# A gated sum formed in TensorE's accumulator banks: two products with the identity per tile in place of a VectorE sum and one transpose

## What is computed

```python
gate = jax.nn.sigmoid(local @ gl_w + remote_h @ gr_w)
mixed = gate * local + (1.0 - gate) * remote_h
mixed = mixed.transpose(0, 2, 1, 3).reshape(B, S, D)
return mixed @ out_w + out_b
```

## Time and profile before

| | |
|---|---|
| median of 3 runs | 1197.87 us (1192.1 to 1199.39) |
| the profiled execution | 1195.67 us, of which the span of instructions is 1193.9 us |
| PE busy (weight loads apart) | 1035.2 us, 87% of the span |
| DVE busy | 930.8 us, 78% |
| POOL busy | 714.8 us, 60% |
| ACT busy | 681.3 us, 57% |
| granted TensorE clock, mean | 0.965 of full speed |
| the chain that ended last | PE 46%, DVE 34%, ACT 8%, issue 6%, POOL 5% |

### The profile page before, as it was taken

The page is one execution under the profiler, slowest core; times in us unless marked ns, Lnnn a source line. Parts: engine busy times, 40 slices in busy tenths (PEclk is TensorE's granted clock), DMA queues, the critical chain, the costliest instruction groups (busy, mean ns, idle before and its releaser), DMA issues.

```text
span 1193.9 us, 38039 instructions
## 1 busy us (share of the span) xinstructions
PE 1035.2 (87%) x15776; PEld 661.3 (55%) x15776; DVE 930.8 (78%) x2148; ACT 681.3 (57%) x1043; POOL 714.8 (60%) x890
## 2 busy tenths in 40 slices
PE   4767899898999999898999989898999989896855
PEld 2435556565656556565656656565655556563533
DVE  5567888889887878879788878888887887975545
ACT  3414566565656566565656566665646656563733
POOL 5406556675656566675665656675655567564744
PEclk9977999999999999999999999999999999996977
DMA  6640241606133250605233160604225060511000
GB/s 219 177 130 3 79 119 41 176 23 166 50 109 91 74 143 32 185 23 145 54 114 103 49 169 32 178 29 126 74 80 137 32 186 23 150 29 39 2 19 18
DMA packets 51272, 108.19 MB, mean 91 GB/s; under 512 B 8054, under 2 KB 35190, under 8 KB 47990
## 3 DMA queue, kind: packets, MB, share of 16 engines
q1 hardware_dynamic: 50460, 105.75, 31.5%
q10 hardware_dynamic: 640, 0.00, 0.0%
HBM read 71.55 MB, written 34.08 MB: 88 GB/s over the span
## 4 chain that ended last, share of the span: by engine, by line
PE 46%; DVE 34%; ACT 8%; issue 6%; POOL 5%; ACTq 0%; DVEq 0%; POOLq 0%
PE oacc L1508 7%; PE oacc L1489 7%; PE work L1565 6%; PE work L1432 5%; PE scores L1469 4%; ACT Pt L793 4%; DVE Pt L979 3%; PE work L1499 3%; DVE nmax L1059 3%; DVE stats L1146 2%; DVE Pt L1017 2%; DVE x L1122 2%; DVE ytok L1140 2%; PE scores L1411 2%; POOL h_lo L664 2%
## 5 line engine op out<-in xcount | busy, mean ns | idle before, releaser
L793 ACT ACTIVATE Pt<-scores 128x1024 f32<-128x1024 f32 (+1 forms) x256 | 228.7, 915 | 116.3 <-PE oacc L1489 75.2
L1059 DVE TENSOR_REDUCE nmax<-work 128x3 f32<-128x480 f32 x352 | 218.2, 637 | 29.5 <-PE work L1437 24.2
L664 POOL TENSOR_TENSOR h_lo<-hbuf,h_hi 128x512 f16<-128x512 f32 x128 | 149.2, 1170 | 133.8 <-DVE h_hi L1181 133.8
L636 POOL TENSOR_SCALAR_AFFINE_SELECT Pt<-Pt 128x512 f32<-128x512 f32 x256 | 166.1, 649 | 95.0 <-ACT Pt L793 93.8
L628 POOL TENSOR_TENSOR parts<-Pt,parts 128x512 bf16<-128x512 f32 x64 | 72.4, 1159 | 142.7 <-ACT parts L743 133.0
L1432 PE MATMUL work<-Ks,Qs 98*32 98x160 bf16 x4096 | 142.0, 236 | 15.2 <-DVE nmax L1059 11.5
L1489 PE MATMUL oacc<-Pt,Vp 128*32 128x256 f32 (+1 forms) x2048 | 149.2, 358 | 4.0 <-POOL Pt L640 3.6
L1508 PE MATMUL oacc<-wdn_t,h_hi 128*128 128x256 f16 x512 | 118.1, 273 | 17.4 <-POOL h_lo L664 17.4
L1469 PE MATMUL scores<-Qs,Ks 100*32 100x160 bf16 (+4 forms) x4096 | 113.9, 228 | 18.9 <-ACT Pt L793 15.9
L640 POOL TENSOR_SCALAR_AFFINE_SELECT Pt<-Pt 128x512 f32<-128x512 f32 x192 | 126.7, 660 | 0.0
L829 ACT ACTIVATE hbuf<-work 128x512 f32<-128x512 f32 x128 | 76.2, 595 | 76.7 <-PE work L1565 61.4
(11 more groups left out here) (169 smaller groups left out, 2078.1 us busy)
## 6 DMA issues: line engine op xcount, KB each, us to landing
parts_scratch<-parts SPq DMA_DIRECT2D x96, 256.0 KB, 5.6
Qs<-parts_scratch SPq DMA_DIRECT2D x96, 256.0 KB, 5.0
Ks<-parts_scratch SPq DMA_DIRECT2D x96, 256.0 KB, 4.7
xtok<-L_attn_x SPq DMA_DIRECT2D x16, 512.0 KB, 6.8
xres<-L_attn_x SPq DMA_DIRECT2D x16, 512.0 KB, 7.7
y<-ytok SPq DMA_DIRECT2D x16, 512.0 KB, 3.3
nat<-L_ffn_w_up SPq DMA_DIRECT2D x1, 1024.0 KB, 8.3
nat<-L_ffn_w_down SPq DMA_DIRECT2D x1, 1024.0 KB, 10.3
```

The source lines that it names most:

```text
L636: ins = pool.affine_select(out=pt[:, :, 0:P], in_=pt[:, :, 0:P], compare_op=ALU.is_gt, fill=0.0, base=0, pattern=[[0, 4], [1, P]], channel ...
L664: pool.tensor_tensor(h_lo[:, t % NR, :], hbuf[:, t % 2, :], h_hi[:, t % NR, :], ALU.subtract).then_inc(h_lo_ready, 1)
L793: nc.scalar.activation(Pt[:, u % NPT, :, 0:w], scores[:, slot, :, :].rearrange("p k (h q) -> p (k h) q", h=2)[:, :, 0:w], ACT.Exp, scale=S ...
L1059: nc.vector.tensor_reduce(nmax[:, :, :].rearrange("p b h -> p (b h)")[:, first:first + n], work[:, slot, 0:n * BAND].rearrange("p (h c) -> ...
```

## The change

VectorE's four sums per sequence are gone, with their semaphore. TensorE waits for `mix_part` in place of `mixed_ready`. For each tile of 128 by 128 it now does two matmuls with the identity as the moving operand, the first with the local part and the second with the remote part as the stationary one. Both go into the same columns of the accumulator: the first with `start=True`, the second adds to it and stops.

```diff
-                    def add_parts(b):
-
-                        dve.wait_ge(mix_part, count(s, NB, b))
-                        nc.vector.tensor_tensor(mixed[:, b, :], mixed[:, b, :], rem[:, s.par, b, 0:D], ALU.add
-                                                ).then_inc(mixed_ready, 1)
-
                     for b in range(NB):
...
-                        if b > 0:
-                            add_parts(b - 1)
-                    add_parts(NB - 1)
...
                     for b in range(NB):
-                        pe.wait_ge(mixed_ready, count(s, NB, b))
+                        pe.wait_ge(mix_part, count(s, NB, b))
                         for t in range(KT):
-                            mm = nc.tensor.transpose(oacc[:, t, b * P:(b + 1) * P],
-                                                     mixed[:, b, t * P:(t + 1) * P], ident[:, :])
+                            cols = slice(t * P, (t + 1) * P)
+                            nc.tensor.matmul(oacc[:, t, b * P:(b + 1) * P], mixed[:, b, cols], ident[:, :],
+                                             start=True, stop=False, skip_group_check=True)
+                            mm = nc.tensor.matmul(oacc[:, t, b * P:(b + 1) * P], rem[:, s.par, b, cols], ident[:, :],
+                                                  start=False, stop=True, skip_group_check=True)
                             if b == NB - 1:
                                 mm.then_inc(mix_T, 1)
```

More of the change, by code:

```diff
@@ L368, in build @@
         xn_lo = sem("xn_lo")
-        mixed_ready = sem("mixed_ready")
         var_ready = sem("var_ready")
```

## The result

| | before | after |
|---|---|---|
| median | 1196.67 us (1192.1 to 1199.39, 4 runs) | 1225.38 us (1221.62 to 1225.78, 4 runs) |
| profiled execution | 1195.67 us, span 1193.9 | 1221.62 us, span 1219.9 |
| PE busy | 1035.2 us | 1071.4 us |
| DVE busy | 930.8 us | 906.3 us |
| chain that ended last | PE 46%, DVE 34% | PE 60%, DVE 23% |

The changed kernel is slower: ratio 1.024 with a 95% interval of 1.020 to 1.028, some 29 us. The forecast was 1229 us, in a range from 1220 to 1246. VectorE has lost the 25 us of work that the change took from it, and TensorE has 36 us more. The profiled execution of the changed kernel is the fastest of its four, so the two traces lie 26 us apart where the medians lie 28.7 apart.

The account below looks back on a forecast made before the run. The chain lay on VectorE, but TensorE's output product reached the residual sum with about 0.1 us slack. 29.5 + 2.5 - 0.6 = 31.4 us on the profiled 1195.67 gives 1227.1, against the median 1229; range 1220 to 1246.

Parts of the forecast that it names:

- VectorE's gain is lost whole: At the residual sum: the 1.34 us per sequence saved on VectorE bring nothing, since it waits 3.7 us for the output product.
- The slack at the meeting point: Where the residual sum needs both VectorE and TensorE's output product: TensorE's side was said to have about 0.1 us.
- the four waits: The residual sum's only waits for the output product before the change, placed in both sums of each of the last two sequences.
- Two passes per product: In MIX_T: each float32 product with the identity takes two passes, so 8 passes become 32, at 0.11 us each.
- The other end, 0.22 per pass: MIX_T's upper bound, weight load and columns one after the other: about 1277 us; part of a rival given 0.13.
- the rival with 0.16: In MIX_T: the load is not fully hidden, a pass costs 0.16 us, total 1251 us; its rival had 0.13.
- the estimate from the Trainium skill: For MIX_T passes: load and matmul pairs about 81 ns apart against 56, so a pass would take an estimated 0.16 us.
- The stage: MIX_T to ScalarE's copies, sequences 1 to 13: first bank complete after the 30th pass, copies 2.29 us later.
- GpSimd's branch: Behind ScalarE's copies: GpSimd's four L628 come 2.29 us later and delay VectorE's small copy L1151; with this, 2.27 per sequence was taken.
- No idle time on the chain in which the shift could vanish: After the residual sum all engines follow at the same distances, so the shift stays: 13 x 2.27 = 29.5 us.
- Sequences 14 and 15: The last two sequences, TensorE's clock low: the new stream brings it back, shortening output products; -0.3 us each, +2.8 as other end.
- The sum: Whole run: 29.5 + 2.5 (sequence 0) - 0.6 (last two) = 31.4 us slower on the profiled execution; the forecast had 0.78.

Follow-up runs that it names:

- the kernel with the unused sum: The changed kernel with VectorE's four sums per sequence put back, written to a tile nobody reads: 1224.47 us, ratio 1.024 to the kernel before.
- the kernel without the sum: The kernel before with VectorE's sum left out and nothing in its place, so the remote part is never added: 1189.06 us, ratio 0.994.
- The kernels with MIX_T early: MIX_T ahead of the last projection, LAT_RQ behind OUT; ratios to before: two adding transposes 0.990, the kernel before 1.002, the change 1.011.
- The kernels with two adding transposes: The changed kernel with both products per tile as transposes, the second adding: 1200.11 us in usual order (ratio 1.003), 1183.83 with MIX_T early (0.990).
- the two later kernels that have the 16 transposes: Two adding transposes with MIX_T early, plus either ScalarE's copies L743 ahead of L736 (1181.43 us, 0.988) or two reductions for VectorE's small instructions (1176.19 us, 0.983).

## Why the prediction was right, step by step

**The direction and its reason.** "VectorE's gain is lost whole" held to a hundredth of a microsecond in the kernel with the unused sum. The slack at the meeting point was smaller still than the 0.1 that the prediction gave it, from the hand-over of sequence 15: by the kernel without the sum it is about 0.01. One reading of the earlier trace rows was wrong and nothing hangs on it: the four waits are the first residual sum of sequence 0 (1.00 us), both of sequence 14 (5.71 and 0.40) and the first of sequence 15 (5.71).

**The number and price of the passes.** Two passes per product and 0.111 us per pass held. The nearest row, L1349, had decided for a load that is hidden although it is as long as the columns; the trace after shows pairs 0.22 apart. The other end, 0.22 per pass, and the rival with 0.16 fell. So did the estimate from the Trainium skill ("TensorE: Matmul & The Clock Gate", Back-to-back issue gap); no run here shows its 81 ns at 128 columns.

**The stage.** Here a term was mis-sized. The prediction let the first bank be complete after the 30th pass. But a tile has two products of two passes, and behind the last tile of the first bank come four passes of the second one, so it is the 28th. 27 x 0.111 + 0.27 + 0.04 = 3.31 is what the trace shows (3.32), not 3.50. The copies came 2.11 later and not 2.29, and the end of the copy L1151 and the second residual sum also 2.11. With 2.11 in place of 2.27 that is 13 x 0.16 = 2.1 us of the sum. The first residual sum came 2.16 later, where 2.17 was said, and this is in part luck: the prediction let the output product follow the copies at the old distance, but it waited for TensorE itself, which had four more passes and LAT_RQ to do. The two errors cancelled. Sequence 0 shifted by 2.8 at the first residual sum and 2.6 at the second, against 2.5.

**GpSimd's branch.** The step said that L1151 waits for the four L628, and took the later branch for that reason. This was the branch that counted: L1151 ended with the last of them before (549.94 and 549.91) and after (564.89 and 564.87). But the reason was wrong in part: it waits for the one in flight, and a reduction in its place doesn't. The kernels with MIX_T early show that moving those four doesn't move the chain by as much.

**What is carried on.** "No idle time on the chain in which the shift could vanish" held in the regular periods: 67.8 us before and 69.9 after, +2.09. But some periods are longer than that in every trace. Those extra stretches add 3.4 us over sequences 0 to 13 in the trace of before and 1.1 in that of after, so the two traces differ by 24.6 us there and not by 27. One such stretch, in sequence 11 of before, lies in the attention half (it arises between 850 and 875 us of the span, where ScalarE and TensorE hand scores and weights to each other). What sets it was not looked into. The medians differ by 28.7, so this is probably a matter of the single execution, which isn't shown.

**Sequences 14 and 15.** Forecast -0.3 each; the shift changed by -1.3 in 14 and by 0.0 in 15 (at the second residual sums). The mechanism held: in 14 the copies came 1.0 us later and 2.3 were given back behind them, in 15 it was 2.0 and 2.0. TensorE starts on the first block's parts, at the low clock, and the stream brings the clock back before it ends (busy time by stretch; the column before the DMA share is the granted clock, 0.50 being 1.2 GHz and 1.00 being 2.4 GHz):

```profile
1112.00:1116.90 4.90, 4.53 (x21) 4.53 (x22) 2.33 (x7) 0.00 (x0) 0.00 (x0) 0.50 0.00 0
1117.00:1119.00 2.00, 1.37 (x13) 1.18 (x11) 0.00 (x0) 1.04 (x2) 0.00 (x0) 1.00 0.00 0
1119.10:1123.00 3.90, 3.72 (x16) 2.96 (x16) 1.69 (x5) 0.00 (x0) 0.00 (x0) 1.00 0.00 0
```

The stream started at 1112.37, so the clock was back after 4.6 us in sequence 14, and after 4.0 in sequence 15. The output products then took 3.72 us in both, against 6.31 and 6.03 before:

```profile
1119.10 3.72 PE L1296 MATMUL work<-wout,mixT 128*128 128x256 f32 x16 [0.73 <-ACT mixT L805]
```

This is the one place where the change gains.

The prediction wondered whether the eight transposes of before failed to bring the clock back because waits broke them. The kernels with two adding transposes bear on it. In sequence 14 of the first two of them, usual order and early, TensorE stood idle for 4.3 us, then ran the 16 transposes one behind the other and nothing else, and the granted clock went from 0.50 to 1.00 after 3.7 and 3.3 us of that, ahead of the output product. So transposes alone were enough there. In sequence 15 of the same kernels the same stream was not followed by it, and the output product took 6.19 and 6.08 us, most of it at the low clock; in the two later kernels that have the 16 transposes the product took 5.6 to 5.8 us in both sequences. What tells these apart stays open.

**The sum.** 31.4 us forecast on the profiled execution. The regular steps that it could see gave 13 x 2.1 + 2.6 - 1.3 = 28.6, which is the difference of the medians; the miscounted passes are most of the rest. The other expectations, in the order of the text: 512 records, a block of 3.73 us where 3.7 was said, L805 released by TensorE 16 times, the period at 69.9 where 70.1 was said. The wait of the residual sum was in 16 instances and 65.9 us, where 18 and above 50 were forecast.

## To carry to other kernels

An instruction on the chain of waits is worth its time only up to the slack of whatever meets the chain next: look where the engine that is relieved next waits, and how late its partner arrives there. Then look for a second meeting point behind the first: here the one that set the period was with GpSimd, and it hid in a small copy that looked busy. To move a float32 sum into the accumulator, use transposes that add, one pass each, and not products with the identity, which take two; and then change the order, so that the engine that gave up work is the one the others wait for. Look for a small VectorE instruction that takes far longer in some instances than in others: beside GpSimd, a one-input reduction didn't wait where a copy did, which was worth 14 us here for two lines. Count passes at the instruction whose end releases the next engine (the 28th of 32 here), and all of them for what TensorE itself does next.

## What the runs showed of the hardware

- A float32 transpose with `start=False` adds to what stands in the accumulator, at 0.11 us per tile of 128 by 128. No row of before showed one that adds.
- A float32 pass hides a weight load that is just as long as its columns (0.11 us, as passes of one column show): 0.111 us per pass at 128 columns, in a row of 32, at the full clock; 0.215 at the low one (two pairs 0.43 apart).
- A two-column copy on VectorE that takes 0.17 us alone took 0.92 to 1.17 beside GpSimd's subtraction L628 of 128 by 512, and ended within 0.04 us of one of these in all ten kernels where it was a copy and stood in their midst, as a two-input form did (0.97). As a reduction it took 0.16. Products and sums of 128 by 256 with both inputs in SBUF took 0.94 in place of 0.42 beside L686.
- Sixteen float32 transposes in a row, with TensorE idle for 4.3 us before them, were followed by the full clock after 3.3 and 3.7 us in sequence 14 of two kernels, and not in sequence 15 of these nor in either sequence of two others.
- Two-input instructions of two columns beside GpSimd's L650 and L656 kept their 0.15 to 0.16 us.
